# A copy of all experts' weights in SBUF, and the tiles' weights copied from it

## The chip, the cores and the metric

The kernel runs on one core of a Trainium2 chip. The time is the device time of one execution in microseconds (us), the median of several runs. A core has five engines with queues of their own: TensorE (PE; its weight loads are shown as PEld), VectorE (DVE), ScalarE (ACT), GpSimd (POOL) and SyncE (SP), which here only issues DMAs. Sixteen DMA engines move data between HBM and SBUF for all queues.

## The reference

The input is 8 x 256 tokens of 128 floats. Six stages follow each other, each adding to the token: glu experts, attention with a sink and a window, the same glu experts again, mlp experts, an RWKV block, the same mlp experts again. An expert stage normalises the token, picks the best two of eight experts by a gate, and mixes their outputs with softmax weights:

```
glu: y_e = ((x W0_e + b0_e) * silu(x W1_e + b1_e)) W2_e + b2_e      x: 128, hidden: 512
mlp: y_e = gelu(x W1_e + b1_e) W2_e + b2_e, besides a shared gelu(x Ws + bs); then a layer norm
out = x + 0.5 * sum over the two chosen experts of weight * y_e
```

## The kernel before, in words

The tokens stay in `x_tok` in SBUF. In an expert stage (`moe_sp`, `moe_pool`, `moe_act`, `moe_pe`, `moe_dve`, one function for each engine's queue) the four blocks of 512 tokens are normalised into `xm_tok` (L294), which SP stores to the HBM tensor `xn_rows` (L322). The gate gives each token two experts. The 4096 (token, expert) pairs are sorted by expert and padded so that every expert begins a new tile of 128 rows; `NTILE` is 39 tiles in every stage. DVE computes `te_i`, the expert of each tile (L609), and then the tables of rows: one-hot matrices `oh_a`, `oh_b` (L621 to L625), multiplied and summed by TensorE (L489, signal `_table`), from which `sidx` and `gidx` come (L628, L629).

The loop over the 39 tiles is pipelined over the engines. POOL gathers 128 rows of `xn_rows` into one of six places `xg` (L348) and scatters the finished rows to `y_rows` (L355). TensorE transposes the gathered tile (L497), ACT copies it to `xt` (L411), TensorE computes the four chunks of the hidden layer (L509 and L512 for glu, L512 for mlp), ACT and DVE apply the nonlinearity (L422, L650), TensorE sums the output over the chunks, three chunks behind (L521), ACT adds the bias into `yt` (L430, signal `_ysb`), TensorE transposes back (L528), DVE copies to `yo` (L657).

The weights of an expert are one row of 1545 floats (glu, 6180 B) or 1029 floats (mlp, 4116 B) on each of 128 partitions, that is 0.791 or 0.527 MB. `tile_weights` (L302) on SP reads the expert's number into a register and loads that expert's set from HBM into place j mod 5 of `wt`. The first five loads wait for `te_i` only; load j waits for `_ysb` of tile j - 5. TensorE waits for the load at the first chunk of tile j (`up`, L503). The order on SP in a stage: the four stores of `xn_rows`, in the first mlp stage the raw RWKV weights (L1082), in the first glu stage two stores of zeros to `v_rows` for the attention (`zero_values`, L315), the 39 loads, a wait for all scatters, the reads of `y_rows` back.

Tensors with different lifetimes lie at the same addresses: `shared_place` allocates its list, frees it again, and the next call begins at the same address.

Of the kernel before, what the change touches and what calls it, by code (L numbers as in the profile page):

```python
# [4 lines left out]
F32 = mybir.dt.float32  # L5
# [7 lines left out]
P = 128  # L13
B, T, D = 8, 256, 128
NT = B * T // P
NBLK = 4
TPB = NT // NBLK
BC = TPB * P
E = 8
# [4 lines left out]
NTILE = (2 * NT * P + E * (TS - 1)) // TS  # L24
NA = -(-NTILE // 2) * 2
SLOTS_BASE = 2 * NT * P
WSLOTS, XSLOTS, PIECES, LAG = 5, 6, 4, 3
BEHIND = 3


GLU_COLS = 3 * 512 + 2 * HC + 1
# [40 lines left out]
def turns_of(slots, i):  # L72

    return len(range(i, NTILE, slots))


def signals_of_one_use(kind, what):
    if kind in ("glu", "mlp"):
        per = {"_up": HC * NTILE, "_act": HC * NTILE, "_hid": HC * NTILE, "_dn": HC * NTILE, "_gT": NTILE, "_xt": NTILE,
               "_ysb": NTILE, "_yT": NTILE, "_yo": NTILE, "_xn_out": 16 * NBLK, "_logits": 1, "_scattered": 16 * NTILE, "_incl": 1, "_offs": 1,  # L80
               "_te": 1, "_onehot": PIECES, "_table": 1, "_idx": 1, "_gap": 1, "_tanh": 1}
        for i in range(WSLOTS):
            per[f"_w_in{i}"] = 16 * turns_of(WSLOTS, i)
        for i in range(XSLOTS):
            per[f"_xg_in{i}"] = 16 * turns_of(XSLOTS, i)
        for b in range(NBLK):
            per[f"_y_in0{b}"] = per[f"_y_in1{b}"] = 16
        return per.get(what, NBLK)
    return NBLK
# [5 lines left out]
class Stage:  # L95
# [11 lines left out]
    def at(self, what, value):  # L107
        return value + (self.moe_use if self.shared(what) else self.use) * signals_of_one_use(self.kind, what)
# [7 lines left out]
def build_program(nc, x_in, glu_pack, glu_gate, glu_gate_b, mlp_pack, mlp_gate, mlp_shared, mlp_rows,  # L116
                  attn_pack, rwkv_pack, rwkv_cols, out, stages=("glu", "attn", "glu", "mlp", "rwkv", "mlp")):
    ctx = ExitStack()
    with ctx:
# [5 lines left out]
        def sem(name):  # L125
            if name not in sems:
                sems[name] = ctx.enter_context(nc.semaphore(name))
            return sems[name]
# [75 lines left out]
        def shared_place(*tensors):  # L204
            with ExitStack() as place:
                return [place.enter_context(nc.sbuf_tensor(n, s, d)) for n, s, d in tensors]

        xm_tok, xT_sb, wt, eq_a, oh_a, oh_b, xg, xt, act_ring, hid, yt, yo, y_in, sh_tok, mix_w, cv_w = shared_place(
            ("xm_tok", [P, NT, D], F32), ("xT_sb", [P, NBLK, BC], F32), ("weights", [P, WSLOTS, GLU_COLS], F32),
            ("eq_a", [P, 2 * NT, NA], F32), ("oh_a", [P, 2 * NT, NA], R32), ("oh_b", [P, 2 * NT, P], R32),  # L210
            ("xg", [P, XSLOTS, D], F32), ("xt", [P, 2, TS], F32), ("act_ring", [P, 4, TS], F32),
            ("hid", [P, 4, TS], F32), ("yt", [P, 2, TS], F32), ("yo", [P, NTILE, D], F32),
            ("y_in", [P, 2, NT, D], F32), ("sh_tok", [P, NT, D], F32),
# [6 lines left out]
            ("scores", [P, 2, 8, KEYS], F32), ("probs", [P, 4, 8, KEYS], F32), ("probsT", [P, 2, 4 * ROWS], F32),  # L220
            ("rowmax", [P, 2, 8], F32), ("rowsum", [P, 2, 8], F32), ("rowinv", [P, 4, 8], F32), ("wo_T", [P, BC], F32))

        zero_rows = y_in[:, 1, 0:2, :].rearrange("p t d -> p (t d)")
        attn_raw = y_in[:, 0, :, :].rearrange("p t d -> p (t d)")[:, 0:OCOL]
        rwkv_in = y_in[:, 0, :, :].rearrange("p t d -> p (t d)")[:, 0:RWKV_COLS]
# [16 lines left out]
        def prepared(n):  # L242

            return n > 0 and order[n][1] == "rwkv" and order[n - 1][1] == "mlp"

        def feeds(n):
            return n + 1 < len(order) and prepared(n + 1)
# [41 lines left out]
        def normalise(v, st, name, src, n, slot=0, dst=None):  # L289

            v.wait_ge(sem(st + name + "_rstd"), st.at(name + "_rstd", n + 1))
            dst = dst or (lambda t: xn_tok[:, slot, t, :])
            for t in range(TPB):
                ins = nc.vector.tensor_scalar(dst(t), src(t), meanvar[:, slot, t, 0:1], rstd[:, slot, t:t + 1],  # L294
                                              ALU.subtract, ALU.mult)
            return ins

        def layernorm(v, st, name, src, n, dst=None):
            moments(v, st, name, src)
            return normalise(v, st, name, src, n, 0, dst)  # L300

        def tile_weights(sp, n, st, m, j):  # L302
            slot = j % WSLOTS
            pack = glu_pack if m.gated else mlp_pack
            if j >= WSLOTS:
                sp.wait_ge(sem(st + "_ysb"), st.at("_ysb", j - WSLOTS + 1))
            e = sp.value_load(te_i[0:1, j:j + 1], min_val=0, max_val=E - 1)
            sp.dma_start(wt[:, slot, 0:m.cols], pack[:, bass.ds(e * m.cols, m.cols)]).then_inc(
                sem(st + f"_w_in{slot}"), 16)

        def zero_values(sp):
            sp.wait_ge(sem("zero_rows_set"), 1)
            runs = 2 * NBLK * 2
            for first, count in ((0, LEFT), (LEFT + T, XAW - LEFT - T)):
                sp.dma_start(bass.AP(v_rows, first * 256, [[XAW * 256, runs], [256, count], [1, 256]]),  # L315
                             zero_rows[0:runs, :].unsqueeze(1).broadcast_to([runs, count, 256])).then_inc(
                    sem("v_zero"), 16)

        def moe_sp(sp, n, st, m):
            for b in range(NBLK):  # L320
                sp.wait_ge(sem(st + "_in_norm"), st.at("_in_norm", b + 1))
                sp.dma_start(xn_dram.ap().rearrange("(t p) d -> p t d", p=P)[:, TPB * b:TPB * (b + 1), :],  # L322
                             xm_tok[:, TPB * b:TPB * (b + 1), :]).then_inc(sem(st + "_xn_out"), 16)
            if feeds(n):
                rwkv_raw(sp)
            if n == 0:
                zero_values(sp)
            sp.wait_ge(sem(st + "_te"), st.at("_te", 1))
            for j in range(NTILE):
                tile_weights(sp, n, st, m, j)  # L330
            sp.wait_ge(sem(st + "_scattered"), st.at("_scattered", 16 * NTILE))
            if n == 0:
                sp.wait_ge(sem("attn_w_ready"), 2 * OCOL // 512)
                sp.wait_ge(sem("v_zero"), 16 * 2)
            if feeds(n):
                sp.wait_ge(sem("rwkv_w_ready"), 11)
            for b in range(NBLK):
                src = y_dram.ap().rearrange("(k t p) d -> p k t d", k=2, p=P)[:, :, TPB * b:TPB * (b + 1), :]
                for k in range(2):
                    sp.dma_start(y_in[:, k, TPB * b:TPB * (b + 1), :], src[:, k, :, :]).then_inc(  # L340
                        sem(st + f"_y_in{k}{b}"), 16)
# [739 lines left out]
        def rwkv_raw(sp):  # L1081
            sp.dma_start(rwkv_in, rwkv_pack).then_inc(sem("rwkv_in"), 16)  # L1082
# [294 lines left out]
        def rwkv_dve(v, n, st, m):  # L1377
# [96 lines left out]
            if not prepared(n):  # L1474
                for i in range(11):
# [43 lines left out]
        parts = {"rwkv": (None, rwkv_sp, rwkv_pool, rwkv_act, rwkv_pe, rwkv_dve),  # L1519
                 "attn": (None, attn_sp, attn_pool, attn_act, attn_pe, attn_dve),  # L1520
                 "glu": (GLU, moe_sp, moe_pool, moe_act, moe_pe, moe_dve),
                 "mlp": (MLP, moe_sp, moe_pool, moe_act, moe_pe, moe_dve)}

        @block.sync
# [152 lines left out]
```

## Time and profile before

| what | value |
|---|---|
| median of 3 runs | 1117.88 us (1116.94 to 1121.6) |
| profiled execution | 1118.18 us, span 1116.4 us |
| PE busy | 797.7 us (71%) |
| DVE, ACT, POOL busy | 538.7, 445.3, 433.3 us |
| DMA, hardware queue q1 | 134.03 MB, 40.6% of 16 engines' span |
| loads `weights<-glu_pack`, `weights<-mlp_pack` | 78 x 772.5 KB, 78 x 514.5 KB |

In order of time the stages are: glu experts to about 190 us, attention to about 410, glu to about 582, mlp to about 780, RWKV to about 890, mlp to the end. An expert stage has a front (normalising, gates, tables) in which TensorE is mostly idle, and the loop of 39 tiles. In the profile by slices each digit is a tenth of busy time in a fortieth of the span (27.9 us). A busy DMA engine is one that has a packet under way, which includes the time in which the packet waits for its data.

### The profile page before, as it was taken

The numbers are of one execution on the slowest core, as the hardware profiler recorded it, in microseconds if no ns is written. First come the engines' busy times: TensorE is split into PE (matmuls) and PEld (weight loads), VectorE is DVE, ScalarE is ACT, GpSimd is POOL, SyncE is SP. The second block draws the span as 40 slices with busy tenths as digits, with TensorE's granted clock in tenths as the row PEclk, the third lists the DMA queues.
The fourth block names the chain that finished last, engine by engine and source line by source line (L and its number), as shares of the span: only waits on it lengthen the run. The fifth ranks groups of instructions, "written<-read, shape, count | busy, mean of one in ns | idle before, by whom it ended". The sixth has DMA issues, their size and how long they took to land.

```text
span 1116.4 us, 17251 instructions
## 1 busy us (share of the span) xinstructions
PE 797.7 (71%) x5220; PEld 680.7 (61%) x5220; DVE 538.7 (48%) x1633; ACT 445.3 (40%) x1259; POOL 433.3 (39%) x448
## 2 busy tenths in 40 slices
PE   0579997378989865899974767774177877777750
PEld 0479997267777645798973566664034555666650
DVE  4734444777656537344447521113889543310117
ACT  0045554144445320455550145553087331265540
POOL 1256663022222210565631066663453210466631
PEclk9999999698989985799995579997598885699995
DMA  4559985362513003598954247775000011477752
GB/s 110 131 177 293 291 271 180 95 152 55 124 42 82 2 9 121 179 291 279 276 174 132 94 114 213 211 207 144 1 0 1 1 30 35 136 212 211 210 162 65
DMA packets 79082, 153.77 MB, mean 138 GB/s; under 512 B 11082, under 2 KB 54035, under 8 KB 78992
## 3 DMA queue, kind: packets, MB, share of 16 engines
q1 hardware_dynamic: 69008, 134.03, 40.6%
q0 software_dynamic: 9984, 18.65, 6.1%
q8 instruction: 43, 0.70, 0.3%
q14 instruction: 47, 0.39, 0.1%
HBM read 134.21 MB, written 20.25 MB: 138 GB/s over the span
## 4 chain that ended last, share of the span: by engine, by line
PE 58%; DVE 24%; issue 7%; DMA 4%; ACT 3%; POOL 3%; SPq 1%; another core or an unknown queue 0%; POOLq 0%; ACTq 0%; DVEq 0%
PE bank L521 14%; PE bank L512 12%; PE bank L509 8%; PE bank L945 2%; DVE stats L281 2%; PE bank L528 2%; PE bank L460 2%; PE bank L935 2%; DVE oh_b L623 2%; PE bank L497 2%; DVE sh_tok L675 2%; PE bank L1270 2%; DVE x_tok L675 2%; PE bank L908 1%; PE bank L477 1%
## 5 line engine op out<-in xcount | busy, mean ns | idle before, releaser
L512 PE MATMUL bank<-xt,weights 128*128 128x128 f32 x1248 | 249.8, 283 | 27.5 <-ACT xt L411 16.6
L521 PE MATMUL bank<-hid,weights 128*128 128x128 f32 x1248 | 245.1, 279 | 11.0 <-ACT hid L422 8.2
L348 POOL DMA_INDIRECT xg<-xn_rows,gidx x156 | 153.1, 982 | 238.7 <-DVE gidx L629 129.9
L512 PEld LDWEIGHTS bank<-xt,weights 128*128 128x128 f32 x1248 | 196.5, 199 | 33.9 <-ACT xt L411 20.3
L521 PEld LDWEIGHTS bank<-hid,weights 128*128 128x128 f32 x1248 | 191.1, 194 | 15.3 <-ACT hid L422 9.5
L355 POOL DMA_INDIRECT y_rows<-yo,sidx x156 | 157.1, 1007 | 91.8 <-issue 56.3
L650 DVE SCALAR_TENSOR_TENSOR hid<-bank,weights,act_ring 128x128 f32<-128x128 f32 x312 | 108.9, 349 | 139.5 <-ACT act_ring L422 83.2
L422 ACT ACTIVATE act_ring<-bank,weights 128x128 f32<-128x128 f32 x312 | 115.8, 371 | 111.1 <-PE bank L512 96.5
L657 DVE COPY yo<-bank 128x128 f32<-128x128 f32 x156 | 44.6, 286 | 213.2 <-remote 127.6
L422 ACT ACTIVATE hid<-bank,weights 128x128 f32<-128x128 f32 x312 | 110.6, 372 | 79.8 <-PE bank L521 51.1
L509 PE MATMUL bank<-xt,weights 128*128 128x128 f32 x624 | 128.8, 289 | 5.8 <-issue 2.5
L269 POOL TENSOR_TENSOR rstd<-var_eps,neghalf 128x4 f32<-128x4 f32 x32 | 34.0, 1062 | 206.0 <-DVE var_eps L286 206.0
L509 PEld LDWEIGHTS bank<-xt,weights 128*128 128x128 f32 x624 | 96.1, 194 | 17.2 <-issue 10.2
L768 POOL TENSOR_TENSOR probs<-probs,rowinv 116x512 f32<-116x512 f32 x36 | 40.4, 1121 | 119.9 <-DVE rowinv L1041 119.9
L411 ACT ACTIVATE xt<-bank 128x128 f32<-128x128 f32 x156 | 42.4, 272 | 82.4 <-PE bank L497 81.0
L430 ACT ACTIVATE yt<-bank,weights 128x128 f32<-128x128 f32 x156 | 58.0, 372 | 16.8 <-PE bank L521 16.7
L453 PE MATMUL bank<-ident,xm_tok 128*128 128x128 f32 x64 | 17.6, 430 | 61.8 <-DVE xm_tok L294 61.8
L497 PE MATMUL bank<-ident,xg 128*128 128x128 f32 x156 | 44.2, 284 | 16.6 <-DMA xg<-xn_rows,gidx 16.6
L528 PE MATMUL bank<-ident,yt 128*128 128x128 f32 x156 | 45.4, 291 | 14.1 <-ACT yt L430 10.4
L453 PEld LDWEIGHTS bank<-ident,xm_tok 128*128 128x128 f32 x64 | 12.2, 228 | 64.0 <-issue 55.2
L489 PE MATMUL bank<-oh_a,oh_b 128*128 128x40 f32 x128 | 30.3, 383 | 26.3 <-DVE oh_a L625 26.3
L489 PEld LDWEIGHTS bank<-oh_a,oh_b 128*128 128x128 f32 x128 | 28.5, 328 | 28.1 <-DVE oh_a L625 28.1
(220 smaller groups left out, 1341.8 us busy)
## 6 DMA issues: line engine op xcount, KB each, us to landing
weights<-glu_pack SPq DMA_DIRECT2D x78, 772.5 KB
weights<-mlp_pack SPq DMA_DIRECT2D x78, 514.5 KB
v_sb<-v_rows SPq DMA_DIRECT2D x48, 180.0 KB, 6.5
y_in<-y_rows SPq DMA_DIRECT2D x32, 256.0 KB, 5.0
xn_rows<-xm_tok SPq DMA_DIRECT2D x16, 256.0 KB, 2.2
v_rows<-vd SPq DMA_DIRECT2D x16, 256.0 KB, 2.8
xg<-xn_rows,gidx POOLq DMA_INDIRECT x156
y_rows<-yo,sidx POOLq DMA_INDIRECT x156
```

The costliest lines, as they stand in the source:

```text
L348: pool.indirect_dma_start(out=xg[:, slot, :], out_offset=None, in_=xn_dram.ap()[:, :], in_offset=bass.IndirectOffsetOnAxis(ap=gidx[:, j:j ...
L355: pool.indirect_dma_start(out=y_dram.ap()[:, :], out_offset=bass.IndirectOffsetOnAxis(ap=sidx[:, j:j + 1], axis=0), in_=yo[:, j, :], in_of ...
L422: act.activation(dst[:, k % 4, :], banks[k % 4][:, 0:TS], m.func, bias=wt[:, j % WSLOTS, m.bias_act + c:m.bias_act + c + 1]).then_inc(sem( ...
L430: act.activation(yt[:, j % 2, :], YD[j % 2], ACT.Identity, bias=wt[:, j % WSLOTS, m.bias_out:m.bias_out + 1]).then_inc(sem(st + "_ysb"), 1)
L489: ins = nc.tensor.matmul(TABLE, oh_b[:, u, :], oh_a[:, u, :], start=u == 0, stop=u == 2 * NT - 1)
L497: nc.tensor.transpose(XT, xg[:, slot, :], ident[:, :]).then_inc(sem(st + "_gT"), 1)
L509: nc.tensor.matmul(banks[k % 4][:, TS:2 * TS], wt[:, slot, c * P:(c + 1) * P], xt[:, j % 2, :], start=True, stop=True)
L512: nc.tensor.matmul(banks[k % 4][:, 0:TS], wt[:, slot, o:o + P], xt[:, j % 2, :], start=True, stop=True).then_inc(sem(st + "_up"), 1)
L521: nc.tensor.matmul(YD[j % 2], wt[:, j % WSLOTS, o:o + P], hid[:, k % 4, :], start=c == 0, stop=c == HC - 1).then_inc(sem(st + "_dn"), 1)
L528: nc.tensor.transpose(YO, yt[:, j % 2, :], ident[:, :]).then_inc(sem(st + "_yT"), 1)
L650: nc.vector.scalar_tensor_tensor(hid[:, k % 4, :], banks[k % 4][:, TS:2 * TS], wt[:, j % WSLOTS, m.bias_lin + c:m.bias_lin + c + 1], act_r ...
L675: ins = nc.vector.scalar_tensor_tensor(onto[:, t, :], y_in[:, k, t, :], w_tok[:, k, t:t + 1], onto[:, t, :], ALU.mult, ALU.add)
```

## The change

At the front of each expert stage SP now loads the sets of all eight experts into `all_w`, 8 x 1545 floats per partition, by eight DMAs behind the four stores of `xn_rows`. `tile_weights` copies the set of tile j from `all_w` to `wt`, SBUF to SBUF, with the address in a register on the source. The ring `wt` has four places instead of five and now lies over `eq_a`, `oh_a` and `oh_b`, so the first copy also waits for the table that is computed from them, besides `te_i` and all eight loads.

```diff
-WSLOTS, XSLOTS, PIECES, LAG = 5, 6, 4, 3
+WSLOTS, XSLOTS, PIECES, LAG = 4, 6, 4, 3
...
-        xm_tok, xT_sb, wt, eq_a, oh_a, oh_b, xg, xt, act_ring, hid, yt, yo, y_in, sh_tok, mix_w, cv_w = shared_place(
-            ("xm_tok", [P, NT, D], F32), ("xT_sb", [P, NBLK, BC], F32), ("weights", [P, WSLOTS, GLU_COLS], F32),
+        eq_a, oh_a, oh_b, xm_tok, xT_sb, all_w, xg, xt, act_ring, hid, yt, yo, y_in, sh_tok, mix_w, cv_w = shared_place(
             ("eq_a", [P, 2 * NT, NA], F32), ("oh_a", [P, 2 * NT, NA], R32), ("oh_b", [P, 2 * NT, P], R32),
+            ("xm_tok", [P, NT, D], F32), ("xT_sb", [P, NBLK, BC], F32), ("all_w", [P, E * GLU_COLS], F32),
...
+        wt, = shared_place(("weights", [P, WSLOTS, GLU_COLS], F32))
...
+        def all_weights(sp, n, st, m):
+
+            pack = glu_pack if m.gated else mlp_pack
+            for e in range(E):
+                cols = slice(e * m.cols, (e + 1) * m.cols)
+                sp.dma_start(all_w[:, cols], pack[:, cols]).then_inc(sem(st + "_weights_in"), 16)
+
         def tile_weights(sp, n, st, m, j):
             slot = j % WSLOTS
-            pack = glu_pack if m.gated else mlp_pack
             if j >= WSLOTS:
                 sp.wait_ge(sem(st + "_ysb"), st.at("_ysb", j - WSLOTS + 1))
             e = sp.value_load(te_i[0:1, j:j + 1], min_val=0, max_val=E - 1)
-            sp.dma_start(wt[:, slot, 0:m.cols], pack[:, bass.ds(e * m.cols, m.cols)]).then_inc(
+            sp.dma_start(wt[:, slot, 0:m.cols], all_w[:, bass.ds(e * m.cols, m.cols)]).then_inc(
                 sem(st + f"_w_in{slot}"), 16)
...
+            all_weights(sp, n, st, m)
             if feeds(n):
                 rwkv_raw(sp)
             if n == 0:
                 zero_values(sp)
+            sp.wait_ge(sem(st + "_table"), st.at("_table", 1))
             sp.wait_ge(sem(st + "_te"), st.at("_te", 1))
+            sp.wait_ge(sem(st + "_weights_in"), st.at("_weights_in", 16 * E))
             for j in range(NTILE):
                 tile_weights(sp, n, st, m, j)
```

## Rows read from the trace of the kernel before

**Rows 1.** The page by slices of 27.9 us (DMA), and its HBM line.
```profile
DMA  4559985362513003598954247775000011477752
HBM read 134.21 MB, written 20.25 MB: 138 GB/s over the span
```
**Rows 2.** Stretches: us; busy PE, PEld, DVE, ACT, POOL; clock; DMA share; GB/s.
```profile
112.00:140.00 28.00, 27.86 (x231) 26.16 (x230) 13.57 (x45) 14.71 (x53) 17.78 (x18) 1.00 0.93 293
1014.00:1042.00 28.00, 21.46 (x166) 19.32 (x167) 2.91 (x10) 16.78 (x57) 17.90 (x18) 1.00 0.73 209
```
**Rows 3.** Waits of PE (us, times, longest): 63:188, then 961:1078.
```profile
PE bank L509 <- ACT xt L411: 2.0, 2, 1.6
...
PE bank L512 <- issue: 6.6, 6, 1.9
PE bank L521 <- issue: 2.1, 4, 0.7
```
**Rows 4.** Stretches in which the first five weight loads run behind each other.
```profile
52.00:57.00 5.00, 4.50 (x20) 4.16 (x19) 4.28 (x7) 0.00 (x0) 0.00 (x0) 1.00 0.99 368
57.00:59.00 2.00, 1.30 (x7) 1.19 (x6) 0.54 (x4) 0.00 (x0) 0.00 (x0) 1.00 1.00 414
```
**Rows 5.** SP's issues up to 35 us, and the stretches of the zeros' stores.
```profile
23.93 10.06 SPq L322 DMA_DIRECT2D xn_rows<-xm_tok  x4
34.03 1.11 SPq L315 DMA_DIRECT2D v_rows<-y_in  x2
...
34.50:36.50 2.00, 2.00 (x12) 2.00 (x11) 0.00 (x0) 0.60 (x1) 1.29 (x2) 1.00 1.00 202
36.50:41.00 4.50, 1.49 (x7) 1.40 (x7) 2.70 (x10) 0.00 (x0) 0.00 (x0) 1.00 0.88 96
```
**Rows 6.** Timeline at the first glu loop's front: start, length, instruction, idle before.
```profile
46.28 0.17 DVE L609 TENSOR_SCALAR te_i<-te_f 1x39 int32<-1x39 f32 x1
47.45 4.86 SPq L308 DMA_DIRECT2D weights<-glu_pack  x5
58.34 0.20 DVE L628 TENSOR_SCALAR sidx<-bank 128x40 uint32<-128x40 f32 x1 [1.99 <-PE bank L489]
62.39 0.48 PE L497 MATMUL bank<-ident,xg 128*128 128x128 f32 x1 [4.08 <-DMA xg<-xn_rows,gidx]
63.23 0.79 PE L509 MATMUL bank<-xt,weights 128*128 128x128 f32 x2 [0.37 <-ACT xt L411]
```
**Rows 7.** Timeline at the front of the last mlp layer.
```profile
913.90 6.44 SPq L322 DMA_DIRECT2D xn_rows<-xm_tok  x4
956.45 0.20 DVE L628 TENSOR_SCALAR sidx<-bank 128x40 uint32<-128x40 f32 x1 [1.99 <-PE bank L489]
961.52 1.23 PE L512 MATMUL bank<-xt,weights 128*128 128x128 f32 x4 [0.37 <-ACT xt L411]
```
**Rows 8.** Tile 2's output, the next load, tile 6's start; stretches of that load.
```profile
77.08 0.38 ACT L430 ACTIVATE yt<-bank,weights 128x128 f32<-128x128 f32 x1
78.78 0.02 SPq L308 DMA_DIRECT2D weights<-glu_pack  x1
83.43 0.49 PE L509 MATMUL bank<-xt,weights 128*128 128x128 f32 x2
...
79.00:79.50 0.50, 0.50 (x7) 0.50 (x6) 0.00 (x0) 0.00 (x0) 0.18 (x1) 1.00 1.23 185
81.00:81.50 0.50, 0.50 (x7) 0.50 (x6) 0.45 (x2) 0.36 (x1) 0.10 (x1) 1.00 0.96 396
82.00:82.50 0.50, 0.50 (x7) 0.50 (x6) 0.00 (x0) 0.00 (x0) 0.41 (x1) 1.00 0.75 275
```
**Rows 9.** DMA issues: KB each, median us from issue to landing.
```profile
y_in<-rwkv_pack SPq DMA_DIRECT2D x1, 768.0 KB, 4.5
```
**Rows 10.** Last mlp loop: tile 34's output and tile 38's start.
```profile
1070.75 0.36 ACT L430 ACTIVATE yt<-bank,weights 128x128 f32<-128x128 f32 x1
1075.01 0.46 PE L512 MATMUL bank<-xt,weights 128*128 128x128 f32 x2
```

More of the change, by code:

```diff
@@ L80, in signals_of_one_use @@
                "_ysb": NTILE, "_yT": NTILE, "_yo": NTILE, "_xn_out": 16 * NBLK, "_logits": 1, "_scattered": 16 * NTILE, "_incl": 1, "_offs": 1,
-               "_te": 1, "_onehot": PIECES, "_table": 1, "_idx": 1, "_gap": 1, "_tanh": 1}
+               "_te": 1, "_weights_in": 16 * E, "_onehot": PIECES, "_table": 1, "_idx": 1, "_gap": 1, "_tanh": 1}
         for i in range(WSLOTS):
```

## The prediction

> **What bounds the kernel now.** I read the page by slices first [rows 1]: one core, 1116.4 us, and DMA engines that look nearly full (9 or 8 tenths) in six slices, all in the expert loops of the two glu layers. That invites the thought that weight traffic is the limit. The stage table says otherwise [rows 2]: in 28 us of a glu loop TensorE is busy 27.86 us with the DMA share at 0.93; in an mlp loop it is busy 21.46 of 28 us, DMA 0.73. Then the waits of TensorE in the loop of the first glu layer [rows 3]: 2.0 us behind ACT's copy of the token tile, 0.4 us for issue in a row left out, and none for a weight transfer, although every `up(j, 0)` waits for one. In the last mlp layer it waits for ACT and for issue (6.6 and 2.1 us), again never for weights. So weights are hidden everywhere; what counts is whether the new copies stay hidden, at the front of each of the four expert layers and in the loops.
>
> **Are the loads at the front hidden?** A glu layer loads 8 x 0.791 MB = 6.33 MB. Five of these same loads run behind each other at 368 GB/s in their middle and 414 at their end [rows 4], so 6.33 MB need 6.33/0.368 = 17.2 us. In layer 0 the SP queue issues the last store of normalised rows at 33.6 (four stores from 23.93, 10.06 us in all) and `zero_values` at 34.03 [rows 5]. The eight loads go between, 0.56 us per issue as for the pair of zeros, faster than the 2 us that each needs to move, so the engines set the pace: 34 + 0.6 + 17.2 = 51.8. The zeros, now behind them, kept the queue full or almost full at 202 and 96 GB/s for 6.5 us [rows 5], which gives 58.3. The table, the last thing the copies wait for, is ready at 58.34 [rows 6] and the first copy comes a microsecond later. Just hidden; with the loads a tenth slower it slips 0.7 us. In the other layers the distance is larger: the mlp load is 4.22 MB, 11.5 us, and from the last store (913.90 + 6.44 = 920.3) to the table at 956.45 there are 36 us [rows 7]. The raw rwkv weights move behind the eight loads of layer 3 and arrive some 12 us later, but DVE touches them from tile 8 of the loop on only, over 60 us (the front and eight tiles of 3 us) after the issue: nothing. SP has nothing else behind these waits than the copies themselves.
>
> **The front of a loop.** Before, weights of five tiles were issued right after `te` (46.28 + 0.17 to the issue at 47.45, 1.0 us of register work on SP) and had landed long before. Now the first copy is issued at the table: 58.34 + 1.0 = 59.4. TensorE needs it at 63.23, which the chain table, index, gather, transpose, `xt` sets [rows 6]; that leaves 3.8 us. Price of a copy of 0.791 MB: the trace has no SBUF to SBUF transfer. Nearest rows: the load issued at 78.78 is seen in the half-microsecond windows to begin slowly (185 GB/s), to run at 396 and to fade at 82.3 (275 GB/s in the last), so 3.5 us [rows 8]; and a lone 768 KB load lands after 4.5 us [rows 9]. If reading SBUF costs what reading HBM costs, the copy is there at 62.9 to 63.9: -0.3 to +0.7 us. I take +0.2. Besides, up to four copies now stand on the engines while the first gathers go through; each gather packet can stand behind one row of weights on its engine (6180 B at 414/16 = 26 GB/s is 0.24 us), once or twice: +0.2. For mlp a copy is 0.264 MB less, 3.5 - 0.264/0.414 = 2.9 us, against 956.45 + 1.0 = 957.5 and 961.52, 4.1 us: hidden, only the gather's +0.3 stays. Later tiles: copies follow each other every 1.9 us (0.791/0.414), tiles every 3.2. Sum of the fronts: 2 x 0.4 + 2 x 0.3 = +1.4 us. Lower bound 0 (the copy lands first and no gather is late), upper bound 4 x 2.5 = +10: reading and writing share a rate (below), which makes the first copy 5.4 us.
>
> **The loop with four places.** A copy for tile j now waits for the output of tile j-4, not j-5. Tile 2's `yt` ends at 77.08 + 0.38 = 77.46, and SP issues 1.3 us later, at 78.78; with four places that issue is the copy for tile 6, whose first matmul starts at 83.43 [rows 8]. 83.43 - 78.78 = 4.65 us, against 3.5 us for the load that was really issued there: 1.15 us of slack, where five places had 4.3. In mlp loops tiles are 3 us apart and a load takes 2.9; only the last four or five tiles, 2.0 us apart, come close: tile 34's `yt` ends at 1071.11, +1.0 is 1072.1, tile 38 starts at 1075.01 [rows 10], 2.9 us against 2.9. Nothing in either, or a tenth or two in these last tiles. If the copy were L us long in a glu loop, with L over 4.65, each tile would lose (L - 4.65)/3, since one stall of s moves four periods by 4s and the releasing output by s. As for the engines: a glu tile asks for 0.791 MB of weights and 0.131 MB of gather and scatter, 2.2 us at 0.42 MB/us in a period of 3.16. The 0.93 of [rows 2] overstates the load, since a packet waiting for its first bytes counts as busy (share 1.23 at 185 GB/s, 79.0 to 79.5 [rows 8]). Engine time is hidden as long as a copied row costs less than about 1.5 times a loaded one ((3.16 - 0.31)/1.9).
>
> On that price the Trainium skill has two statements. *DMA: Bandwidth & Descriptors*, "Where 436 GB/s comes from", says that an SBUF to SBUF transfer is limited by the fabric, 435 GB/s; an estimate from it is 1.82 us per glu set, and the sum stays. The trace agrees as far as it goes (414 GB/s in its best stretch [rows 4]), but only with HBM on one side. *SBUF — State Buffer*, "SBUF: two separate sides", gives this peak for a door "alone, one direction", which leaves open what a copy does that reads and writes there at once; that is the first rival.
>
> **Sum.** Profiled execution 1118.18 us (span 1116.4), +1.4: 1119.6; the median of the runs is 0.3 lower, so **1119.5 us**. I choose the engine rate of loads for copies because packets that read SBUF in this trace (the scatters beside the weights) leave the loop's TensorE 99% busy.
>
> **Rivals.**
> (a) A copied row costs twice a loaded one, since one engine reads and writes the same partition through one place. For: nothing here excludes it; against: scatters read SBUF while loads write it, and the loop shows no stall. Then a glu tile needs 3.77 + 0.31 = 4.1 us of the engines against 3.16, 78 tiles x 0.92 = +72; mlp 2.5 + 0.31 = 2.8 under 3.0, nothing; fronts 2 x 2 = +4: 1194 us. It decides from 1.5 times on.
> (b) The ring of four is too short: the copy is somewhat slower (L about 5.5 us, or SP's issue is later with a register in the SBUF address). 78 x (5.5 - 4.65)/3 = +22, fronts +3: 1143 us. It decides from L = 4.65.
> (c) The fronts cost more than their terms: loads or zeros not through when the table is ready, the first tiles' gathers each late by more than a packet, four times +3 us: 1130 us.
> (d) Faster: 24.5 MB per glu layer (39 x 0.791 - 6.33; 16.3 per mlp) no longer read from HBM, so gathers, scatters and instruction loads come back sooner, and the mlp loop gives up some of the 6.5 us in 28 in which TensorE idles. Half of its issue waits (6.6 + 2.1 us in the last layer [rows 3]) over two layers is -9: 1110 us. Against: the glu loop with more traffic has no such stalls, so they are hardly traffic's.
>
> **Chances.** Forecast 0.57, (a) 0.15, (b) 0.10, (c) 0.10, (d) 0.08. One measurement of this kernel tells about 0.5% (5.6 us) from no change. Faster: (d) and a trace of the forecast, 0.09. Slower: (a), (b), most of (c) and the upper edge of the forecast (fronts at +6 or more), 0.38. Same: 0.53. The range, 1113 to 1150, leaves out (a) and the half of (d) below 1113; the forecast's own range is 1116 to 1126.
>
> **What would show it.** Right: TensorE's waits in glu loops still without a weights row, the glu period still 3.16 us, first matmul of a layer 4.9 to 5.6 us behind the table, HBM reads down from 134 MB [rows 1] to 53 (102.8 MB of weight loads less, 21.1 more). Wrong: L509 or L512 waiting for `weights` in every tile, a DMA share near 1 in the loop at a lower rate (a), or copies that begin on an idle engine and end late (b); a first matmul over 6 us behind the table (c).

## The result and the profile after

The changed kernel takes 1131.05 us in the median of four runs (1128.0 to 1138.29), the kernel before, beside it, 1118.39 us (1116.94 to 1121.6). The ratio is 1.0119, 95% interval 1.0066 to 1.0171: 12.7 us slower. The forecast was 1119.5 us, +1.1 against the median shown; the time lies in the range given (1113 to 1150) and near the price of rival (c), 1130.

The profiled execution of the changed kernel took 1138.29 us (span 1136.5), the longest of its four. Its span is 20.1 us over that of before, so the sum of the two traces is larger than what the medians differ by; the experiments below give a closer pair. First its page by slices and its HBM line, against [rows 1].

```profile
DMA  3767775362522006777855155554000013455552
...
HBM read 52.50 MB, written 20.25 MB: 64 GB/s over the span
```

HBM reads fell from 134.21 to 52.5 MB, as forecast, and the DMA digits of the glu loops from 9 and 8 to 7 (one slice has 8). The kernel is slower all the same. Next the front of the first glu layer (timeline: start, length, instruction, idle before it and what ended that), against [rows 6].

```profile
33.92 4.84 SPq L308 DMA_DIRECT2D all_w<-glu_pack  x8
...
58.23 0.20 DVE L638 TENSOR_SCALAR sidx<-bank 128x40 uint32<-128x40 f32 x1 [1.99 <-PE bank L499]
59.13 5.65 SPq L315 DMA_DIRECT2D weights<-all_w  x4
59.54 1.20 POOL L358 DMA_INDIRECT xg<-xn_rows,gidx  x1 [23.79 <-DVE gidx L639]
63.99 0.47 PE L507 MATMUL bank<-ident,xg 128*128 128x128 f32 x1 [5.79 <-DMA xg<-xn_rows,gidx]
64.83 0.79 PE L519 MATMUL bank<-xt,weights 128*128 128x128 f32 x2 [0.37 <-ACT xt L421]
```

The table is ready at the same time (58.23, before 58.34), so the eight loads and the zeros are through. But the first gathered tile is transposed 5.79 us after TensorE's last work, not 4.08, and the first matmul on weights starts 6.60 us behind the table, not 4.89. It is the gather that comes late, not the first copy. The stretches show it (us; busy PE, PEld, DVE, ACT, POOL; clock; DMA share; GB/s): first the eight loads, then the first copy.

```profile
34.50:51.00 16.50, 5.28 (x26) 5.09 (x25) 11.41 (x36) 0.81 (x2) 1.26 (x1) 1.00 1.01 386
51.00:57.00 6.00, 5.50 (x25) 5.16 (x25) 5.18 (x8) 0.00 (x0) 0.00 (x0) 1.00 0.63 132
60.00:60.50 0.50, 0.00 (x0) 0.00 (x0) 0.00 (x0) 0.00 (x0) 0.50 (x1) 1.00 0.45 185
60.50:61.00 0.50, 0.00 (x0) 0.00 (x0) 0.00 (x0) 0.00 (x0) 0.24 (x1) 1.00 0.97 408
61.50:62.00 0.50, 0.00 (x0) 0.00 (x0) 0.00 (x0) 0.00 (x0) 0.50 (x1) 1.00 1.02 396
62.00:62.50 0.50, 0.00 (x0) 0.00 (x0) 0.00 (x0) 0.00 (x0) 0.20 (x1) 1.00 0.56 198
62.50:63.00 0.50, 0.00 (x0) 0.00 (x0) 0.00 (x0) 0.00 (x0) 0.50 (x1) 1.00 0.93 230
```

The loads run at 386 GB/s (the forecast took 368) and are done at 51. The first copy starts between 60.0 and 60.5, runs at about 400 GB/s and fades at 62.2 or so: landed 3.3 us after its issue at 59.13, where the forecast took 3.5. The gather was issued at 59.54, before any byte of the copy had moved, and its packets come only behind it, in the stretch from 62.5. Front of the last mlp layer, against [rows 7]:

```profile
970.68 0.20 DVE L638 TENSOR_SCALAR sidx<-bank 128x40 uint32<-128x40 f32 x1 [1.99 <-PE bank L499]
971.34 4.70 SPq L315 DMA_DIRECT2D weights<-all_w  x4
976.03 0.48 PE L507 MATMUL bank<-ident,xg 128*128 128x128 f32 x1 [5.38 <-DMA xg<-xn_rows,gidx]
976.87 1.22 PE L522 MATMUL bank<-xt,weights 128*128 128x128 f32 x4 [0.37 <-ACT xt L421]
```

6.19 us from table to first matmul, before 5.07. Last, rows of the waits of TensorE over the whole execution (us in all, times, longest), and one of these waits in the timeline.

```profile
PE bank L531 <- ACT hid L432: 24.3, 27, 1.5
PE bank L507 <- DMA xg<-xn_rows,gidx: 21.9, 4, 5.8
...
PE bank L519 <- issue: 6.3, 10, 1.3
PE bank L522 <- issue: 4.8, 5, 2.1
```
```profile
768.68 0.46 PE L522 MATMUL bank<-xt,weights 128*128 128x128 f32 x2 [2.06 <-issue]
```

The four first gathers cost 21.9 us; before it was 16.6 (`L497`, all four). So 5.3 us of the loss sit in one row. No row names weights, and yet TensorE waits for them: the profile shows such a wait mostly as "issue". By the times of the DMA packets, the last byte of the copy for the tile above landed at 767.97, 0.7 us ahead of its first matmul. Counting the tiles whose copy lands less than 0.75 us ahead of their first matmul, the changed kernel has 17 in the glu loops and 6 in the mlp loops, with 13.3 us of idle TensorE just before these matmuls; the kernel before has 5, with no idle time. A table by stage, read off the timelines of each execution, puts the loss in its place: front is table to first matmul on weights, loop is from there to the last `yt`.

| us | fronts, glu, glu, mlp, mlp | loops, glu, glu, mlp, mlp |
|---|---|---|
| before | 4.89 4.85 4.99 5.08 | 125.3 126.2 117.3 117.1 |
| after | 6.60 6.20 6.17 6.19 | 125.5 126.5 124.8 121.8 |

Fronts +5.4, glu loops +0.5, mlp loops +12.2: 18.0 of the 20.1. The other 2 lie in the attention stage (last `yt` of the first glu loop to the second table), which the change does not touch; in the closer pair below they are absent. The first mlp loop, 7.5 us longer, is also disturbed by the clock: TensorE was granted 0.94 of full speed over it (0.98 before), with three stretches of 3.4 us at the lower level (0.5, 1.2 of 2.4 GHz), the last of them from 769.9 on, just behind the stop of 2.06 us above.

### The profile page after: what moved, and what is told of

Read it like the earlier page. It is cut to its first block, busy times and chain, and to the rows that moved or that the text cites. A ratio compares the mean times of both kernels' runs of the same rounds, so it can differ in the third digit from the quotient of the medians.

```text
span 1136.5 us, 17129 instructions
## 1 busy us (share of the span) xinstructions
PE 805.9 (71%) x5220; PEld 690.3 (61%) x5220; DVE 540.7 (48%) x1633; ACT 447.0 (39%) x1259; POOL 433.9 (38%) x448
## 4 chain that ended last, share of the span: by engine, by line
PE 58%; DVE 23%; issue 6%; DMA 4%; ACT 4%; POOL 3%; SPq 1%; another core or an unknown queue 0%; POOLq 0%; ACTq 0%; DVEq 0%
PE bank L531 15%; PE bank L522 13%; PE bank L519 7%; PE bank L955 2%; DVE stats L282 2%; PE bank L470 2%; PE bank L538 2%; PE bank L945 2%; DVE oh_b L633 2%; PE bank L507 2%; DVE sh_tok L685 2%; DMA y_in<-y_rows 1%; PE bank L918 1%; DMA xg<-xn_rows,gidx 1%; PE bank L487 1%
## 5 line engine op out<-in xcount | busy, mean ns | idle before, releaser
L531 PE MATMUL bank<-hid,weights 128*128 128x128 f32 x1248 | 251.2, 285 | 34.1 <-ACT hid L432 24.3
L531 PEld LDWEIGHTS bank<-hid,weights 128*128 128x128 f32 x1248 | 194.4, 197 | 44.3 <-ACT hid L432 30.1
L522 PEld LDWEIGHTS bank<-xt,weights 128*128 128x128 f32 x1248 | 199.6, 202 | 14.1 <-issue 5.7
L432 ACT ACTIVATE act_ring<-bank,weights 128x128 f32<-128x128 f32 x312 | 115.5, 371 | 103.6 <-PE bank L522 87.5
L519 PEld LDWEIGHTS bank<-xt,weights 128*128 128x128 f32 x624 | 96.3, 195 | 16.9 <-issue 8.3
L507 PE MATMUL bank<-ident,xg 128*128 128x128 f32 x156 | 44.7, 286 | 21.9 <-DMA xg<-xn_rows,gidx 21.9
L463 PEld LDWEIGHTS bank<-ident,xm_tok 128*128 128x128 f32 x64 | 12.2, 228 | 64.0 <-issue 55.1
```

The costliest lines, as they stand in the source:

```text
L432: act.activation(dst[:, k % 4, :], banks[k % 4][:, 0:TS], m.func, bias=wt[:, j % WSLOTS, m.bias_act + c:m.bias_act + c + 1]).then_inc(sem( ...
L507: nc.tensor.transpose(XT, xg[:, slot, :], ident[:, :]).then_inc(sem(st + "_gT"), 1)
L519: nc.tensor.matmul(banks[k % 4][:, TS:2 * TS], wt[:, slot, c * P:(c + 1) * P], xt[:, j % 2, :], start=True, stop=True)
L522: nc.tensor.matmul(banks[k % 4][:, 0:TS], wt[:, slot, o:o + P], xt[:, j % 2, :], start=True, stop=True).then_inc(sem(st + "_up"), 1)
L531: nc.tensor.matmul(YD[j % 2], wt[:, j % WSLOTS, o:o + P], hid[:, k % 4, :], start=c == 0, stop=c == HC - 1).then_inc(sem(st + "_dn"), 1)
```

## The experiments

Two theories. A: first gathers wait behind a whole copy, and a ring of four is too short for the mlp loop. B, its rival for the loops: the copies themselves lengthen them, whatever the ring. One fact orders the reading: the kernel before takes 1054 us on one of the chips used and 1110 to 1118 on the others, so each run is compared only with the kernel before on its own chip. 

**e1, e2, e3, e4, on the chip where before takes 1054.37 us.** e1 keeps the late issue behind the table and the ring of four, and takes each tile's set from HBM:

```diff
-            all_weights(sp, n, st, m)
-            sp.dma_start(wt[:, slot, 0:m.cols], all_w[:, bass.ds(e * m.cols, m.cols)]).then_inc(
+            sp.dma_start(wt[:, slot, 0:m.cols], pack[:, bass.ds(e * m.cols, m.cols)]).then_inc(
```

> The changed kernel with the same ring of four in the same place and the same wait for the table, but each tile's set comes from HBM as before and the eight loads at the front are gone. Theory T1 (the first gathers stand behind whole sets of weights on the DMA engines, because the first four transfers now start at the table instead of at the tile numbers): the source doesn't matter, the four fronts are late by 1 to 2 us each, together +5 to +7 us. Theory T2 (the copies themselves, SBUF to SBUF, lengthen the mlp loops): the mlp loops are as long as before, so only the fronts are left, 1123 to 1126 us. Theory T3 (four places are too few): the same length as the changed kernel, 1129 to 1133 us, with the mlp loops 4 to 7 us longer than before.

Measured: 1095.82 us, ratio 1.0395 (1.0367 to 1.0422). Fronts 8.20, 8.23, 7.30, 7.77: 31.5 us in all, where the changed kernel has 25.2 and e2, with early loads, 19.8. So the source does matter, against the first theory of the expectation: the late issue hurts more when the transfer reads HBM; a copy in its place is the milder one.

e2 is the kernel before with the ring alone changed:

```diff
-WSLOTS, XSLOTS, PIECES, LAG = 5, 6, 4, 3
+WSLOTS, XSLOTS, PIECES, LAG = 4, 6, 4, 3
```

> The kernel before with a ring of four places instead of five and nothing else. T1 and T2: no change, 1117 to 1120 us. T3 (four places are too few for the mlp loops): +5 to +8 us, 1123 to 1127 us, and the mlp loops longer by 3 us or more each.

Measured: 1079.2 us, ratio 1.0252 (1.0213 to 1.0291), fronts unchanged (5.00, 4.72, 5.01, 5.05). Waits of TensorE in the first mlp loop, 640 to 740 us:

```profile
PE bank L512 <- issue: 13.6, 29, 1.0
```

In 100 us and some 38 tiles TensorE stops 29 times in front of its first matmul on weights, with no engine to name, and the last bytes of each load land 0.4 to 0.5 us before the tile starts: the wait for weights, shown as issue. The mlp period is 2.62 and 2.55 us here.

e3 is the changed kernel with five places (and a wait for the last store of rows, since the fifth place lies over `xm_tok`):

```diff
-WSLOTS, XSLOTS, PIECES, LAG = 4, 6, 4, 3
+WSLOTS, XSLOTS, PIECES, LAG = 5, 6, 4, 3
+            sp.wait_ge(sem(st + "_xn_out"), st.at("_xn_out", 16 * NBLK))
```

> The changed kernel with a ring of five places (it lies over the normalised tokens too, so the first copy also waits for their stores). T1: fronts as in the changed kernel, table to first matmul 6.2 to 6.6 us. T2: 1129 to 1133 us, nothing gained. T3: the mlp loops back at their length before, 1123 to 1126 us.

Measured: 1057.1 us, ratio 1.0029 (1.0013 to 1.0045). Fronts as in the changed kernel (6.64, 6.51, 6.17, 6.17). Stretches of the mlp loop of e2, then of e3:

```profile
660.00:700.00 40.00, 34.05 (x277) 31.97 (x278) 7.39 (x26) 27.39 (x91) 30.72 (x31) 1.00 0.86 254
```
```profile
650.00:690.00 40.00, 37.68 (x322) 37.33 (x321) 8.36 (x29) 32.31 (x108) 30.64 (x31) 0.96 0.80 286
```

With five places TensorE is busy 37.7 of 40 us and the period is 2.24 us in this stretch; with four 34.1. On this chip the ring decides for loads: +25 us for the fifth place taken away. Copies with five places cost 2.7 us in all, fronts included; copies with four places, the changed kernel itself, were not run here.

e4 cuts each copy of the changed kernel into four DMAs of a quarter of the row:

```diff
+            step = (m.cols + WCUTS - 1) // WCUTS
+            for lo in range(0, m.cols, step):
+                size = min(step, m.cols - lo)
+                sp.dma_start(wt[:, slot, lo:lo + size], all_w[:, bass.ds(e * m.cols + lo, size)]).then_inc(
+                    sem(st + f"_w_in{slot}"), 16)
```

> The changed kernel with each tile's copy issued as four DMAs of a quarter of the columns each. If the first gather waits for the whole DMA in front of it, it now waits for a quarter: table to first matmul 5.1 to 5.6 us instead of 6.2 to 6.6, fronts -4 us in total. If the engines take the two queues in turns of a fixed size whatever the DMA, the fronts stay. Four times as many issues on SP (0.5 us each) may make each copy late by 1 us or more: 1124 to 1140 us.

Measured: 1177.88 us, ratio 1.1176 (1.115 to 1.1202). Front of its first glu layer:

```profile
56.91 0.20 DVE L642 TENSOR_SCALAR sidx<-bank 128x40 uint32<-128x40 f32 x1 [1.99 <-PE bank L503]
...
57.81 8.42 SPq L319 DMA_DIRECT2D weights<-all_w  x10
58.23 1.20 POOL L362 DMA_INDIRECT xg<-xn_rows,gidx  x1 [23.79 <-DVE gidx L643]
...
61.51 0.48 PE L511 MATMUL bank<-ident,xg 128*128 128x128 f32 x1 [4.64 <-DMA xg<-xn_rows,gidx]
...
63.26 0.77 PE L523 MATMUL bank<-xt,weights 128*128 128x128 f32 x2 [1.27 <-DMA weights<-all_w]
```

The gather is back by 1.15 us (4.64 against 5.79): from issue to its last byte 2.9 us, in the changed kernel 4.0. So what stands ahead of a gather is one whole DMA, and its length counts. But now the weights are late: four short copies take longer than one long one. The loops take 3.59 us a tile in the glu layers and 3.39 in the mlp layers, up to 0.9 us for each DMA, though a quarter row keeps its DMA engine for 0.066 us only and eight of them for 0.5. Much of that is the issue: SP issues the quarters of a tile 0.63 to 0.70 us apart, so the last one leaves about 2 us behind the first.

**e5, e6, e7, e8, on a chip where before takes 1110.02 us.** e5 and e6 are the changed kernel and the kernel before once more, with their traces from one chip.

> The changed kernel unchanged, beside the experiments, since the kernel before ran 1054 us there. If the copies (3.3 to 3.8 us from issue to landing) are shorter than the loads (4.2 to 4.8 us) with the same ring of four, this stands between the ring of five with copies (1057 us) and the ring of four with loads (1079 us): about 1065 to 1072 us, with the loops waiting for the landing of each set in the glu layers. If four places cost nothing with copies: 1057 us. If the source doesn't matter: 1090 to 1096 us, as with the late loads.

> The kernel before, for its profile beside the experiments: 1050 to 1058 us; glu period about 2.9 us and mlp period about 2.3 us a tile, weights landing 2 us or more ahead of their tile.

e5: 1124.05 us, ratio 1.0120 (1.0097 to 1.0142). e6, one execution: 1109.93 us. Both expectations, and the times in that of e7, were written for the chip with 1054 us and say nothing of this one.

e7 takes the front away: five places, over `xm_tok` and `xT_sb` first, so that two are free at `te`; two copies are issued there, the others when the first gathered tile has been transposed.

```diff
-            sp.wait_ge(sem(st + "_table"), st.at("_table", 1))
+            sp.wait_ge(sem(st + "_xn_out"), st.at("_xn_out", 16 * NBLK))
...
             for j in range(NTILE):
+                if j == 2:
+                    sp.wait_ge(sem(st + "_gT"), st.at("_gT", 1))
```

> Copies with a ring of five that lies over the normalised tokens first, so that tiles 0 and 1 are copied as soon as the tile numbers and the eight loads are there, and the copies from tile 2 on wait for the transpose of the first gathered tile. Theory T1 (the late copies hold back the first gathers): table to first matmul back to 4.9 to 5.1 us in all four layers, 5 to 6 us less than the ring of five alone: 1050 to 1053 us, under the kernel before by 1 to 4 us. If the fronts' loss has another cause (more traffic of any kind before the gathers): 1056 to 1058 us.

e8 is e7 with six places.

> The same with six places. If five places still make tiles wait for landings (the mlp layers with copies had as little as 0.5 us between landing and first use), 2 to 6 us less than with five, and mlp periods nearer to 2.1 us. If the ring no longer limits: the same as with five within 1 us.

e7: 1116.19 us, ratio 1.0055 (1.0038 to 1.0073). e8: 1117.44 us, ratio 1.0065 (1.0047 to 1.0084). Front of e7's first glu layer:

```profile
54.30 10.13 SPq L316 DMA_DIRECT2D weights<-all_w  x4
57.59 0.20 DVE L641 TENSOR_SCALAR sidx<-bank 128x40 uint32<-128x40 f32 x1 [1.99 <-PE bank L502]
61.60 0.47 PE L510 MATMUL bank<-ident,xg 128*128 128x128 f32 x1 [4.05 <-DMA xg<-xn_rows,gidx]
62.44 0.79 PE L522 MATMUL bank<-xt,weights 128*128 128x128 f32 x2 [0.37 <-ACT xt L424]
```

4.05 us for the gather, 4.85 from table to matmul, as before the change. The four executions by stage:

| us | fronts | loops | span |
|---|---|---|---|
| e6 (before) | 4.89 4.66 4.92 5.03 | 123.9 125.0 115.5 115.1 | 1108.2 |
| e5 (after) | 6.38 6.20 6.18 6.18 | 124.4 126.1 121.8 119.3 | 1125.7 |
| e7 | 4.85 4.69 4.90 5.03 | 124.3 125.0 120.1 118.3 | 1114.7 |
| e8 | 4.94 4.68 4.89 5.02 | 125.9 125.5 119.0 119.4 | 1115.7 |

e5 against e6 closes: fronts +5.4, glu loops +1.6, mlp loops +10.5, sum 17.5, spans 17.5 apart. e7 takes back the 5.4 of the fronts, 1.2 of the glu loops and 2.7 of the mlp loops, and keeps 7.8 in the mlp loops. None of its copies there lands less than 1.0 us ahead of its tile, in e8 none less than 2.0, and a sixth place gives nothing more. In e5 25 tiles of all four loops have their copy land less than 0.75 us ahead. The mlp loops cut in three (first matmul to the fourth `yt`, thirty more, the last five) show what the ring has a part in: both together take 32.9, 179.2 and 18.5 us in e6, 32.4, 185.4 and 23.3 in e5, 34.9, 184.8 and 18.7 in e7. The fifth place returns the whole 4.8 us of the last five tiles, where four places were too few; e7 pays 2.0 us of its own in the first four, for a reason not looked into; and in the thirty between them a loss of about 6 us stays with five places (5.6) and with six (6.0, e8). So theory A accounts for the fronts, for most of the glu loss and for nearly half of the mlp loss; the 6 us look like B.

**e9, e10, e11, on a chip where before takes 1116.92 us.** The test of B: e9 is e7 with copies in the glu layers alone, e11 is e7 with loads from HBM in all layers and no `all_weights`, e10 is the kernel before with six places.

```diff
+            src = all_w if m.gated else mlp_pack
-            sp.dma_start(wt[:, slot, 0:m.cols], all_w[:, bass.ds(e * m.cols, m.cols)]).then_inc(
+            sp.dma_start(wt[:, slot, 0:m.cols], src[:, bass.ds(e * m.cols, m.cols)]).then_inc(
```

> The early ring of five places, with copies from SBUF in the two glu layers and loads from HBM, without the eight loads at the front, in the two mlp layers. Theory M (copies lengthen the mlp loops by themselves, also where no tile waits for a landing): where the kernel before takes 1110 to 1118 us, the mlp loops go back from 118 to 120 us to 115 to 117, and the time is the kernel before's within 3 us. Rival (the different places and waits, not the copies, cost the mlp loops their 3 to 5 us): the mlp loops stay at 118 to 120 us, +5 to +7 us. If the kernel before takes 1054 us, as it did beside the first four experiments, the mlp loops show no loss from copies and both agree.

> The kernel before with a ring of six places and nothing else. If five places already keep every landing ahead of its tile, no change (within 3 us). If the landings still limited a loop (where the kernel before takes 1054 us, loads took 4.2 to 4.8 us and four places cost 25 us), 3 to 8 us less.

> The same early ring of five and the same waits, with loads from HBM in all four layers and no loads at the front. Theory M: mlp loops as in the kernel before and the total its time within 3 us; glu loops the same as with copies within 1 us. Rival (places and waits cost it): +5 to +7 us, as with the early copies.

e9: 1118.28 us, ratio 1.0018 (1.0006 to 1.003); loops 127.1, 126.9, 117.4, 116.9. e11: 1117.75 us, ratio 1.0013 (0.9996 to 1.0031); loops 125.4, 127.5, 117.6, 117.5. e10: 1116.59 us, ratio 1.0004 (0.9991 to 1.0016); loops 125.0, 126.4, 117.2, 116.4. Only mlp copies are missing in e9, and the mlp loss is gone; in e11 the glu copies go as well, and nothing more comes back. The thirty tiles take 182.2 us in e9, 182.4 in e11 and 182.0 in e10, the kernel before but for its ring. B holds, with one gap: no kernel with mlp copies ran on this chip, so each side is held against the kernel before on its own chip. The copies themselves lengthen the mlp loop by some 6 us for the pair, and leave the glu loop nearly alone (254.0 for the two of e9, 252.9 in e11, 251.3 in e10). e10 also bears on theory A: in its glu layers the sixth load is still under way when the first gather is issued (408 GB/s from 59 to 60 us, gather issued at 58.23), TensorE waits 5.10 us for that gather, not 4.08, and the fronts are 5.91 and 5.42; its mlp fronts are 5.02 and 5.14. So a load ahead of the gather does the same as a copy. First e10's first transposed tile; then the same 80 us of mlp loop in e11, e9 and e10, and on the other chip in e6 and e7:

```profile
61.98 0.48 PE L497 MATMUL bank<-ident,xg 128*128 128x128 f32 x1 [5.10 <-DMA xg<-xn_rows,gidx]
```

```profile
665.00:745.00 80.00, 60.66 (x470) 54.52 (x470) 10.25 (x37) 46.15 (x155) 51.81 (x52) 1.00 0.75 212
```
```profile
665.00:745.00 80.00, 60.98 (x466) 54.42 (x466) 9.96 (x36) 45.90 (x153) 51.90 (x52) 1.00 0.76 211
```
```profile
665.00:745.00 80.00, 60.42 (x466) 54.32 (x466) 9.96 (x36) 45.41 (x154) 51.98 (x52) 1.00 0.76 212
```
```profile
665.00:745.00 80.00, 60.81 (x473) 54.85 (x472) 10.23 (x37) 47.09 (x157) 52.35 (x53) 1.00 0.76 212
```
```profile
665.00:745.00 80.00, 60.10 (x461) 53.62 (x460) 9.96 (x36) 44.48 (x153) 50.63 (x52) 1.00 0.58 206
```

With copies the DMA share is 0.18 lower and yet fewer tiles pass: 461 matmuls in e7 against 473 in e6. So it is no contention for DMA engines, and the clock is at 1.00 in all five. What goes along with it stands on DVE and ACT. Scatters, DVE's copies of the output, and ACT's and TensorE's next work in the last mlp loop, first of e6, then of e7:

```profile
1005.69 1.02 POOL L355 DMA_INDIRECT y_rows<-yo,sidx  x1 [0.30 <-issue]
1007.51 0.29 DVE L657 COPY yo<-bank 128x128 f32<-128x128 f32 x1 [4.25 <-remote]
1007.56 0.37 ACT L422 ACTIVATE hid<-bank,weights 128x128 f32<-128x128 f32 x1 [1.10 <-PE bank L521]
...
1008.14 0.49 PE L512 MATMUL bank<-xt,weights 128*128 128x128 f32 x2 [1.15 <-ACT xt L411]
...
1011.75 1.02 POOL L355 DMA_INDIRECT y_rows<-yo,sidx  x1 [0.31 <-issue]
1013.58 0.29 DVE L657 COPY yo<-bank 128x128 f32<-128x128 f32 x1 [4.26 <-remote]
```
```profile
1007.25 1.02 POOL L368 DMA_INDIRECT y_rows<-yo,sidx  x1 [0.30 <-issue]
...
1009.32 0.63 ACT L435 ACTIVATE hid<-bank,weights 128x128 f32<-128x128 f32 x2 [2.26 <-PE bank L525]
1009.39 0.29 DVE L670 COPY yo<-bank 128x128 f32<-128x128 f32 x1 [4.76 <-remote]
...
1009.74 0.49 PE L534 MATMUL bank<-hid,weights 128*128 128x128 f32 x2 [1.33 <-ACT hid L435]
...
1013.63 1.02 POOL L368 DMA_INDIRECT y_rows<-yo,sidx  x1 [0.30 <-issue]
1015.80 0.29 DVE L670 COPY yo<-bank 128x128 f32<-128x128 f32 x1 [4.46 <-remote]
```

In about 15 of 39 mlp tiles DVE stands idle until 1.8 us (e6) or 2.1 us (e7) behind the issue of a scatter, then writes `yo`; POOL's next work waits for that. The hold is not DVE's alone: ACT stands idle too and begins within 0.11 us of DVE in all 29 such places of e6 and in 22 of 23 of e7, though in the rows of e7 the last matmul ahead of it ended at 1008.40, and TensorE waits for ACT behind it. So the hold lies on the path of the loop. Two tiles take 6.06 us in these rows of e6 and 6.38 in those of e7. Counting holds of over 1.5 us behind the scatter's issue, their mean over a loop is 1.88 to 2.00 us in e6, e9, e10 and e11, and 2.07 to 2.15 in e5, e7, e8 and e12; in the first pair of traces it is 1.97 and 1.98, then 2.25 and 2.26: longer with mlp copies in every case. An estimate from these: 0.2 us more in each of some 26 holds of both loops is about 5 us, near the 6 that are to be explained. On the chip where before takes 1054 us there is no such hold at all. That it carries this part of the mlp loss is likely and not shown; what holds DVE and ACT there, and why a copy prolongs it, is open and was not tried by itself.

**e12, on a further chip where before takes 1110.3 us**, is e3 again, to see whether its near parity was the chip's.

> The changed kernel with a ring of five, again, because its first timing was made where the kernel before takes 1054 us. Where the kernel before takes 1110 to 1118 us: fronts as in the changed kernel (6.2 to 6.4 us), mlp loops 118 to 121 us, the ratio to the kernel before 1.009 to 1.012 (the changed kernel 1.012, the early ring 1.0055: of the 6.8 tenths of a per cent between them the fronts' 5.5 us are 5). If the fifth place is what the mlp loops miss: 1.005 or less with fronts unchanged. Where the kernel before takes 1054 us: 1.003 as before.

Measured: 1119.11 us, ratio 1.0082 (1.0063 to 1.0101); fronts 6.53, 6.35, 6.16, 6.18, loops 123.9, 124.8, 118.4, 117.1. The near parity was the chip's. The mlp loops together, 235.5 us, are 5.6 shorter than in e5 (241.1) on a chip of nearly the same speed: the last five tiles take 18.4 us, as with early copies, and the thirty before them 185.8. So the fifth place is worth about half of the mlp loss also when the copies start late, more than the 2.7 us that e7 alone suggests. None of the versions tried beats the kernel before by more than a measurement tells; e10 and e11 equal it.

## Why the prediction was right and wrong

The time lies in the stated range because that was drawn wide for the rivals, which is luck as far as the mechanism goes: the forecast's own range, 1116 to 1126, does not hold it, and the sum of +1.4 us was wrong in two places, the fronts and the mlp loops.

**Hidden loads: right.** Loads through at 51 (forecast 51.8), table at 58.23, no slip in any layer. The HBM term too (52.5 MB, forecast 53).

**Price of a copy: right; rival (a) falls.** A copied row of 6180 B keeps its DMA engine 238 ns in the median and 245 in the mean; a loaded one in the glu loops before 236 and 306: the same in the median, with more long ones among the loads. A copy is landed 3.3 us after its issue when alone. On the glu loops the forecast of nothing nearly stands, with +0.5 (+1.6 in e5 against e6). But the 1.15 us of slack are used up: in 12 of their 78 tiles TensorE stands idle until the copy has landed (12 in e5), and e7 with five places returns 1.2 of the 1.6 us.

**The gather's term: wrong, and the step that failed in the fronts.** "Each gather packet can stand behind one row of weights on its engine ..., once or twice: +0.2." It stands behind the whole rest of the copy ahead of it. A copy is eight rows on each engine (128 rows on 16), 8 x 0.24 = 1.9 us for glu and 8 x 0.16 = 1.3 for mlp. The first gather took 2.4 us from issue to last byte before and 4.0 after: its first packet started 1.9 us behind the issue before and 3.0 after, at 62.52, just when the copy's last row had landed (62.43). Measured +1.71, +1.35, +1.18 and +1.11 instead of 2 x 0.4 + 2 x 0.3: +5.4, not +1.4. Shown from three sides: a shorter DMA ahead gives back 1.15 us (e4), none ahead gives back everything (e7), and a sixth load ahead costs the kernel before 1.0 us of its first front (e10). The Trainium skill has the rule, *DMA: Bandwidth & Descriptors*, "Queues, rings and completion order": an engine takes turns between its queues by packet, and a packet in that sense is typically a bundle of some 9 to 17 descriptors, not a row. The trace agrees in kind: the turn lasted a copy's whole share of eight rows. The forecast took the rows of the trace for the unit of turns.

**The mlp loops: wrong, the larger half.** "Nothing in either, or a tenth or two in these last tiles." Measured +12.2 in the first pair, +10.5 in e5 against e6, and it has two parts.

The last five tiles: +4.8 us (+5.5 in the first pair), returned by a fifth place (e7, e8, e12). The forecast held 2.9 us against 2.9 here. In its sum the copy is issued 1.0 us behind the `yt` that frees its place, takes 2.9, and TensorE starts with its last byte. Tile 36 of e5's last loop shows the three terms: `yt` of tile 32 ends at 1075.31, the copy is issued at 1076.59, its last byte lands at 1079.82 and the first matmul starts at 1080.41, so 1.3, 3.2 and 0.6 us. The step that failed is this slack: the way from the freeing `yt` to the matmul takes 5.1 us, not 3.9, and its last term, from last byte to matmul, was put at nothing.

The thirty tiles before them: +6.2 us, which no place returns and which goes only with the copies (e9, e11). Here the slack for the weights was large enough. But [rows 2] showed TensorE busy for 21.46 of 28 us in this loop: something else sets its pace, and the forecast never named it. So it could not say what a slower link there costs. Which link it is stays open; the hold of DVE and ACT behind the scatters grows with copies by about as much. Rival (d) had looked at the same idle time and expected gain from less HBM traffic; scatters did come back sooner (mean 2.5 to 2.7 us from issue to last byte in mlp loops, before 3.5), and no time came of it.

**Rival (b), the short ring,** was right in kind and wrong in its place. It priced the glu loops at +22, where four places cost 1 to 2 us, and left out the last mlp tiles, where they cost 5. It is larger on the faster chip, where it costs e2 25 us. There the forecast's bookkeeping holds once the missing term is in: four periods must hold a tile from first matmul to `yt` (4.8 us in e2's mlp loops), 0.7 us to the issue, the load (4.2 to 4.4 us to landing) and 0.5 from landing to matmul, 10.3 us, so 2.6 a tile; measured 2.62 and 2.55. Where a loop takes 3.1 us a tile anyway that is no bound, where it could run at 2.24 it is.

**Rival (c)** gave 1130 us by fronts alone, 4 x 3. The total is close by chance: fronts cost 5.4, and the mlp loops the rest. Its mark, a first matmul over 6 us behind the table, was seen in all four layers. The evidence in hand for the gather's term was one rate; its upper bound should have been one whole transfer in each layer, 2 x 1.9 + 2 x 1.3 = 6.4 us, and the value nearer to that than to a row.

## What to carry to other kernels

Bytes and rate are not the whole price of a transfer that is moved in time: ask which small transfer of another queue is issued just behind it, and charge that one the length of the whole DMA ahead of it. Judge the depth of a ring at the period of the loop where that is shortest (here its last tiles), with the time from last byte to first use in the sum, and on the fastest chip that the kernel meets. That no row of the waits names a tensor does not say that nobody waits for it: hold the last byte of its transfer against its first use. In a loop where no engine is full, find the chain that sets its pace before calling an edit free; traffic taken off HBM buys nothing if that chain does not run through it.

## What the runs showed of the hardware

A copy from SBUF to SBUF keeps a DMA engine as long as a load from HBM (238 and 236 ns for 6180 B, stretches at 396 to 408 GB/s). The Trainium skill, *DMA: Bandwidth & Descriptors*, "Where 436 GB/s comes from", puts such transfers at the fabric's 435 GB/s, and the trace comes near it. But its first packet starts 0.66 to 0.79 us after the end of the issuing instruction, a load's after 0.34 to 0.43 (medians of the loops, transfers that had no other ahead of them). Changed kernel, in its first glu loop, a copy's issue and the stretches behind it:

```profile
72.99 0.49 SPq L315 DMA_DIRECT2D weights<-all_w  x1
...
73.50:74.00 0.50, 0.50 (x7) 0.50 (x6) 0.25 (x1) 0.22 (x1) 0.00 (x0) 1.00 0.01 0
74.00:74.50 0.50, 0.50 (x7) 0.50 (x6) 0.32 (x2) 0.39 (x2) 0.15 (x1) 1.00 0.89 371
```

Nothing moves in the half microsecond from 73.5 on, and at 74 the copy runs at once at 371 GB/s. Copies issued behind each other hardly overlapped (the share falls to 0.56 between the first two, from 62.0 to 62.5 above; the second's first row came 0.4 us behind the first's last). From a transfer's last byte to the first matmul on it 0.4 to 0.7 us passed where it stood waiting (e2, e5).

And the same kernel takes 1054 us on one chip and 1110 to 1118 on the others. The changed kernel with five places runs its mlp tiles in 2.24 us there (e3) and in over 3 elsewhere, and costs 0.3% there and 0.8% on another chip (e12).
